# Slots zeroed during the scan, four tiles' statistics at its end, and a re-ordered attention head

## The reference, cut to what matters

```python
x = x + tanh(g_xattn[0]) * mamba(ctx, layernorm(x))     # selective scan, 512 channels x 16 states
x = x + tanh(g_ffn[0])   * moe(layernorm(x))            # 16 experts, top 2, and a shared expert
x = x + tanh(g_xattn[1]) * attention(layernorm(x), ctx) # 32 heads of 16, rotary positions, Wout
x = x + tanh(g_ffn[1])   * ffn(layernorm(x))            # both weights rounded to -1, 0, 1
```

## Time and profile before

| | us |
|---|---|
| three runs, median (lowest to highest) | 1593.91 (1592.81 to 1600.19) |
| the profiled execution | 1594.93 |
| its span, first to last instruction | 1593.1 |
| PE, DVE, ACT, POOL busy | 1457.8, 1136.2, 969.9, 531.4 |

### The profile page before, as it was taken

How to read it: one execution, slowest core, us unless ns; L and a number is a source line. 1 busy time by engine, 2 the same in 40 slices (tenths; PEclk the granted TensorE clock), 3 DMA queues, 4 the chain that set the end, 5 groups by cost and what they waited for, 6 DMA issues and landing times. The chain is left out here.

```text
span 1593.1 us, 21411 instructions
## 1 busy us (share of the span) xinstructions
PE 1457.8 (92%) x6233; PEld 635.7 (40%) x6245; DVE 1136.2 (71%) x1673; ACT 969.9 (61%) x1527; POOL 531.4 (33%) x343
## 2 busy tenths in 40 slices
PE   5788988889978999999999788899999999989999
PEld 2334434444434444444444343332333333334444
DVE  7899999999995422222223757788989999737885
ACT  3999999999934011111111532477787887877764
POOL 0679788698961630000003645705000000000000
PEclk7799989989989999999999889999999999999999
DMA  5202102003473484457524626354323233120464
GB/s 188 64 25 58 49 21 74 20 15 80 151 245 141 165 219 156 145 203 263 187 90 139 219 80 178 117 181 122 81 72 95 72 84 83 59 106 14 81 140 123
DMA packets 141799, 183.41 MB, mean 115 GB/s; under 512 B 54771, under 2 KB 88947, under 8 KB 140707
## 3 DMA queue, kind: packets, MB, share of 16 engines
q1 hardware_dynamic: 120198, 134.58, 28.7%
q0 software_dynamic: 6624, 23.14, 4.7%
q10 hardware_dynamic: 14912, 24.89, 4.7%
HBM read 109.29 MB, written 54.92 MB: 103 GB/s over the span
## 5 line engine op out<-in xcount | busy, mean ns | idle before, releaser
L1814 DVE TENSOR_REDUCE a_mx<-a_s 128x2 f32<-128x1024 f32 x256 | 303.5, 1218 | 33.9 <-PE a_s L1928 30.4
L267 POOL TENSOR_TENSOR m_hs<-m_hs,m_C 128x1024 f32<-128x1024 f32 x128 | 302.2, 2379 | 74.9 <-DVE m_hs L474 74.4
L474 DVE TENSOR_TENSOR_SCAN m_hs<-m_dA,m_d 128x512 f32<-128x512 f32 x256 | 293.4, 1199 | 6.9 <-PE m_d L625 6.1
L625 PE MATMUL m_d<-ident_sb,m_dBuT 128*128 128x128 f32 x1024 | 161.8, 290 | 25.1 <-DVE m_hs L474 20.7
L625 PEld LDWEIGHTS m_d<-ident_sb,m_dBuT 128*128 128x128 f32 x1024 | 116.9, 146 | 153.6 <-DVE m_hs L474 86.3
L373 ACT ACTIVATE m_dA<-m_dt,m_negA 128x512 f32<-128x512 f32 x256 | 168.2, 711 | 6.3 <-DVE m_hs L474 3.8
L1252 PE MATMUL e_gu<-e_w,e_xgT 128*128 x376 | 169.1, 592 | 0.0
L351 ACT ACTIVATE m_dBuT<-m_dtuT,m_BT 128x512 f32<-128x512 f32 x241 | 157.8, 711 | 0.1
L1928 PE MATMUL a_s<-ring_sb 96*128 96x512 bf16 x512 | 150.8, 384 | 5.7 <-DVE a_mx L1814 4.7
L920 ACT ACTIVATE e_sg<-e_gu 128x256 f32<-128x256 f32 x47 | 18.0, 383 | 222.9 <-PE e_gu L1252 222.9
L640 PE MATMUL m_y<-m_hs,m_fold 128*64 128x512 f32 x512 | 142.9, 639 | 0.4 <-POOL m_hs L267 0.4
(11 more groups left out here) (329 smaller groups left out, 2424.1 us busy)
## 6 DMA issues: line engine op xcount, KB each, us to landing
e_w<-in_ex_gu SPq DMA_DIRECT2D x16, 1024.0 KB, 6.2
ring_sb<-qk_dram SPq DMA_DIRECT2D x64, 192.0 KB, 3.1
xg_dram<-zeros_sb SPq DMA_DIRECT2D x2, 6016.0 KB, 28.3
e_xg<-xg_dram ACTq DMA_DIRECT2D x47, 256.0 KB, 2.7
yg_dram<-attn_sb ACTq DMA_DIRECT2D x47, 256.0 KB, 2.0
m_C<-c_dram SPq DMA_DIRECT2D x64, 128.0 KB, 2.9
m_dt<-m_dt SPq DMA_DIRECT2D x64, 128.0 KB, 2.3
e_w<-in_ex_dn SPq DMA_DIRECT2D x16, 512.0 KB, 7.6
```

The lines of the kernel that those rows point to most:

```text
L267: pool.tensor_tensor(hs[:, J % RH], hs[:, J % RH], C2[:, N % RC].unsqueeze(1).broadcast_to([P, 2, L]), ALU.mult).then_inc(s_hc, 1)
L474: dve.tensor_tensor_scan(hs[:, J % RH, h], dA[:, j % RA], pd[j % RD][:], 0.0, ALU.mult, ALU.add)\
L625: last = pe.transpose(pd[j % RD][:, t * P:(t + 1) * P], dBuT[:, N % 2, t, g], ident[:])
L1814: dve.tensor_reduce(mx[:, r % 2, h * TB + 2 * c:h * TB + 2 * c + 2], psc[c][:], AX.X, ALU.max)\
```

## The change

1. **Zeros.** The two DMAs behind the last C load are gone. From the fifth `load_c` on, each is followed by one or two DMAs that zero one slot (256 KB) each, 47 in all over 28 loads. POOL's wait before the scatter counts 47 DMAs.
2. **First chunk's layer norm.** At the end of `mamba`'s list ACT sums the four tiles of batch 0 (Identity with an accumulated output), negates and scales the sums to minus the mean, sums squares of x - mean, and takes the root; DVE adds a reciprocal and a product ahead of its last gate and add. `moe` takes these columns: ACT begins with the four normalisations, DVE with the statistics of tiles 4 and 5, and copies of chunk 0 alternate with the statistics of 6 and 7; `columns(1)` moves ahead of the statistics of 8 and 9.
3. **Shared weights.** One semaphore for each of the three; PE waits for gate, up and down where each is first used.
4. **Attention head.** POOL's inverse roots of batches 0 and 1 follow the gathers of tiles 7 and 11. `inverse(3)` stands ahead of `rotate(0)` on DVE, `normalise(3)` ahead of item 0 on ACT, the turning of batch 3 at n = 1 on PE.
5. **First maxima.** DVE splits them, right behind the last maxima of the group (n = 8 and n = 12), with the `split` that its loop already uses. At n = 10 PE projects the first half, turns the maxima, projects the second half, and then waits for the turned maxima's copy.

```diff
             def load_c(N):
 ...
+                if N == RC:
+                    sp.wait_ge(s_z0, 1)
+                for j in range(zeroed(N), zeroed(N + 1)):
+                    sp.dma_start(xg_dram[j].rearrange("p (c d) -> p c d", c=2),
+                                 zeros[:].unsqueeze(1).broadcast_to([P, 2, D // 2])).then_inc(s_zero, 16)
+            def zeroed(N):
+                return max(N - RC, 0) * ST // (B * PAIRS - RC)
 ...
-            for c in range(2):
-                sp.dma_start(xg_dram.rearrange("j p d -> p j d")[:, :, c * D // 2:(c + 1) * D // 2],
-                             zeros[:].unsqueeze(1).broadcast_to([P, ST, D // 2])).then_inc(s_zero, 16)
 ...
+            act.wait_ge(s_add, E4)
+            for t in range(TB):
+                if t >= 1:
+                    act.wait_ge(s_lead, t)
+                act.activation(junk[:], x_sb[:, t], ACT.Identity, accum_out=lead[:, 0, t:t + 1]).then_inc(s_lead, 1)
+            act.wait_ge(s_lead, TB)
+            act.activation(lead[:, 0], lead[:, 0], ACT.Copy, scale=-1.0 / D).then_inc(s_lead, 1)
+            for t in range(TB):
+                act.wait_ge(s_lead, TB + t + 1)
+                act.activation(junk[:], x_sb[:, t], ACT.Square, bias=lead[:, 0, t:t + 1], accum_out=lead[:, 1, t:t + 1])\
+                    .then_inc(s_lead, 1)
+            act.wait_ge(s_lead, 2 * TB + 1)
+            act.wait_ge(s_eps, 1)
+            act.activation(lead[:, 1], lead[:, 1], ACT.Sqrt, scale=1.0 / D, bias=lead[:, 2, 0:1]).then_inc(s_lead, 1)
 ...
             for et in range(E4 - 1):
                 add(B - 1, et)
+            dve.wait_ge(s_lead, 2 * TB + 2)
+            dve.reciprocal(lead[:, 1], lead[:, 1]).then_inc(s_lead, 1)
+            dve.wait_ge(s_lead, 2 * TB + 3)
+            dve.tensor_tensor(lead[:, 0], lead[:, 0], lead[:, 1], ALU.mult).then_inc(s_lead, 1)
             gate_sum(B - 1, E4 - 1)
 ...
-            root(0)
-            normalise(0)
+            for t in range(TB):
+                act.activation(xn[:, t], x_sb[:, t], ACT.Identity, scale=lead[:, 1, t:t + 1], bias=lead[:, 0, t:t + 1])\
+                    .then_inc(s_xn, 1)
 ...
-            statistics(0, 1, 2, 3)
-            variance(0)
-            columns(0)
             statistics(4, 5)
-            copy_x(0, 1, 2, 3)
-            statistics(6, 7)
+            copy_x(0)
+            statistics(6)
+            copy_x(1)
+            statistics(7)
+            copy_x(2)
             variance(1)
+            copy_x(3)
+            columns(1)
             statistics(8, 9)
-            columns(1)
 ...
-            pe.wait_ge(s_ws, 16 * 3)
+            pe.wait_ge(s_ws[0], 16)
             shared_block(0, 0)
             turn_x(4, 5)
             turn_logits(0)
+            pe.wait_ge(s_ws[1], 16)
             shared_block(0, 1)
 ...
-                if t in (8, 12):
-                    inverse_root(t // TB - 2)
+                if t in (7, 11):
+                    inverse_root(t // TB - 1)
 ...
-                if n in (FIRST + 4, FIRST + 8):
-                    split((n - FIRST - 4) // G4)
 ...
+            normalise(3)
             for n in range(ITEMS - 1):
-                if n == 1:
-                    normalise(3)
 ...
             variance(3)
+            inverse(3)
             rotate(0)
-            inverse(3)
 ...
                     maxes_of(0, g, h, 1)
+                    if h == G4 - 1:
+                        split(0, g)
 ...
                 if n == 1:
                     turn_x(2)
-                if n == 2:
                     turn_x(3)
 ...
+                project(n, 0)
                 if n == FIRST + 5:
                     pe.wait_ge(s_zero, 1)
                     pe.wait_ge(s_mx, 9)
                     turn(0, 0, pmt_early)
-                project(n, 0)
-                if n == FIRST + 5:
+                    project(n, 1)
                     pe.wait_ge(s_mc, 1)
```

More of the change, by code:

```diff
@@ L33, with mamba @@
 LN_READY = 2 * NT + 3
-def mamba(nc, x_sb, ident, identb, tg, a, c_dram, xg_dram, zeros, s_zero):
+def mamba(nc, x_sb, ident, identb, tg, a, c_dram, xg_dram, zeros, s_zero, lead):
     G8 = 2 * E4
@@ L61, in mamba @@
         w_xp = sb("w_xp", [P, E4, RX])
+        junk = sb("junk", [P, D])
         w_dt = sb("w_dt", [R, D])
@@ L102, in mamba @@
         s_cst = sem("c_stored")
+        s_eps = sem("epsilon_set")
+        s_lead = sem("first_layer_norm_steps")
         s_d2 = [sem(f"dt_doubled{i}") for i in range(E4)]
@@ L231, in _ @@
             pool.memset(zeros[:], 0.0).then_inc(s_z0, 1)
+            pool.memset(lead[:, 2], EPS).then_inc(s_eps, 1)
             def scale_first(et):
@@ L712, with moe @@
 GR = 8
-def moe(nc, x_sb, ident, tg, a, xg_dram, yg_dram, s_zero, early, s_early, attn, s_tab, slot, wk, tab_dram, yo, s_yst):
+def moe(nc, x_sb, lead, ident, tg, a, xg_dram, yg_dram, s_zero, early, s_early, attn, s_tab, slot, wk, tab_dram, yo, s_yst):
     with ExitStack() as ctx:
@@ L794, in moe @@
         s_wg = sem("gate_weights_loaded")
-        s_ws = sem("shared_weights_loaded")
+        s_ws = [sem(f"shared_{n}_loaded") for n in ("gate", "up", "down")]
         s_pad = sem("gate_weights_padded")
@@ L840, in _ @@
             sp.dma_start(iota[:], a["iota"].partition_broadcast(P)).then_inc(s_w, 16)
-            sp.dma_start(ws2[:], a["sh_down"].rearrange("(k p) e -> p k e", p=P)).then_inc(s_ws, 16)
+            sp.dma_start(ws2[:], a["sh_down"].rearrange("(k p) e -> p k e", p=P)).then_inc(s_ws[2], 16)
             def load_expert(e, r):
@@ L898, in _ @@
             pool.wait_ge(s_slot, 1)
-            pool.wait_ge(s_zero, 32)
+            pool.wait_ge(s_zero, 16 * ST)
             for k in range(2):
@@ L924, in root @@
             def root(c):
-                act.wait_ge(s_var, c + 1)
+                act.wait_ge(s_var, c)
                 act.activation(rstd[:, c * TB:(c + 1) * TB], rstd[:, c * TB:(c + 1) * TB], ACT.Sqrt).then_inc(s_sd, 1)
             def normalise(c):
-                act.wait_ge(s_nm, c + 1)
+                act.wait_ge(s_nm, c)
                 for t in range(c * TB, (c + 1) * TB):
@@ L1023, in columns @@
                 r = rstd[:, c * TB:(c + 1) * TB]
-                dve.wait_ge(s_sd, c + 1)
+                dve.wait_ge(s_sd, c)
                 dve.reciprocal(r, r).then_inc(s_ln, 1)
@@ L1289, in _ @@
             shared_up(3)
+            pe.wait_ge(s_ws[2], 16)
             for n in range(4, NB):
@@ L1631, in part_3 @@
                     .then_inc(s_p3, 1)
[L1633 to L1644, removed]
             for n in range(2):
@@ L2026, in _ @@
                     scores(0, g, h, 0)
-                project(n, 1)
+                if n != FIRST + 5:
+                    project(n, 1)
                 if 0 <= g < 2:
@@ L2515, in build @@
         s_zero = ctx.enter_context(nc.semaphore("slots_zeroed"))
-        mamba(nc, x_sb, ident, identb, tg, a, c_dram, xg_dram, zeros, s_zero)
+        lead = ctx.enter_context(nc.sbuf_tensor("lead_sb", [P, 3, TB], F32))
+        mamba(nc, x_sb, ident, identb, tg, a, c_dram, xg_dram, zeros, s_zero, lead)
         early = ctx.enter_context(nc.sbuf_tensor("early_sb", [P, KD * T], F32))
@@ L2520, in build @@
         yo = attn[:].rearrange("p i t c -> p (i t c)")[:, (NT - 2) * D:NT * D].rearrange("p (a d) -> p a d", a=2)
-        moe(nc, x_sb, ident, tg[:, 2:3], a, xg_dram, yg_dram, s_zero, early, s_early, attn, s_tab, slot, wk, tab_dram, yo, s_yst)
+        moe(nc, x_sb, lead, ident, tg[:, 2:3], a, xg_dram, yg_dram, s_zero, early, s_early, attn, s_tab, slot, wk, tab_dram, yo, s_yst)
         mark = ctx.enter_context(nc.semaphore("first_after_moe"))
```

6 lines of the change are left out of this document (2 added, 4 removed).

## The result

The changed kernel took 1584.61 us (median of 7 runs, 1582.01 to 1589.26); the kernel before, in the same group, 1597.01 (7 runs, 1592.81 to 1600.59). The ratio is 0.9928, 95% interval 0.9909 to 0.9946: 0.7% faster, where 1.0% was forecast. The profiled execution took 1584.61 us with a span of 1582.6, against 1594.93 and 1593.1: 10.3 us by the times and 10.5 by the spans, where the sum said 16.2. In medians the gain is 12.4 us. The forecast of 1577.7 was counted from 1593.9, the median of three runs of the kernel before; in this group that kernel took 3.1 us more.

The account below looks back on a forecast made before the run. DVE and ACT nearly fill the scan; elsewhere PE sets the pace, losing time idle and at half clock. Terms +0.3 -4.2 (including +0.4) -3.3 -5.8 -3.2 = -16.2 us from 1593.9 gave 1577.7, say 1578; range 1569 to 1590.

Parts of the forecast that it names:

- Zeros in the scan: Scan's batch borders: 256 KB zeros delay ACT 1.3 us three times, mostly covered by slack; +0.3 us, bounds 0 and 4.
- The slack of 6.5 us: Scan: ACT made the decays by 161.5, DVE needs them only at 167.98, so later ACT copies would mostly be absorbed.
- Statistics: Scan's end: ACT's early sums hidden in its free time, DVE's two small instructions not hidden; +0.4 us, bounds 0 and 1.0.
- Expert head: Expert block's start: earlier normalisation and turning, logits at 472.7, shared block at 474.6, clock rising near 477; -4.2 us.
- Rival (d): Expert and attention heads: PE's clock stays at 2.4 GHz in both, giving 1571 us; chance 0.09.
- Attention head: Attention block's start to item 2: earlier roots and batch 3 turning bring item 2's rotation forward; -3.3 us, bounds 0 and -6.4.
- The tie at the first operand load: Attention head: item 1's operand load lands at 944.4 as PE reaches first scores at 944.3; 0.3 us charged.
- Items 8 to 15: Attention items: DVE's split costs 0.72 us and is ready early, removing PE's gaps at n = 10 (-5.8) and 14 (-3.2).
- the bound of -6 for the pair: n = 10 and 14 together: smallest gain, if DVE's added work and item 10's chain eat a third; other bound -10.2.
- Rival (a): Attention head and items: waits return at the first operand load (+3) and n = 10 (+3), giving 1584 us; chance 0.19.
- Rival (b): SP's queue at scan borders: dt2 copies held behind zeros, 21 us per border, giving 1641 us; chance 0.07.
- rival (c): Scan and both heads: ACT stays 4 us behind, heads give less, no change that shows, 1589 us; chance 0.15.

Follow-up runs that it names:

- again: The changed kernel itself, unaltered, timed once more in a later group as yardstick: median 1597.29 us, 0.9909 of the kernel before.
- a_fill: Changed kernel, but POOL's two subtractions beside each early split of maxima only write zeros: one execution 1589.39 us, kernel before 1612.23.
- a_late: Changed kernel, each early split behind the next item's rotation, PE projecting both halves of items 10 and 14 before the turning: one execution 1588.84 us, before 1612.23.
- a_pool: Changed kernel with the early splits back on POOL, PE's new order at item 10 kept: one execution 1595.27 us, kernel before 1612.23.
- after: First profiled execution of the changed kernel, all parts of the change in: 1584.61 us against 1594.93 for the kernel before.
- x_lead: Kernel before plus only the early statistics, the expert head using them and separate shared-weight waits: one execution 1602.25 us, kernel before 1614.04.
- late5: Same code as a_late, timed against the kernel before: median 1591.79 us, ratio 0.9871.
- late_zend: late5 with the slots zeroed in two large DMAs at the scan's end: median 1588.47 us, 0.9861 of the kernel before.

## Why the forecast held, and where its working was wrong

**Zeros in the scan (+0.3).** The cost at a border was right: 0.60 us of issue, 1.3 us more wait on average over three (1.1, 0.9, 2.0). What it does to the end was not: starts with zeros (8 kernels, 466.65 to 469.44) average 467.75, without (5, 465.76 to 467.26) 466.50, so about 1.2 us. With a scatter as wide as that the mean is weak evidence for the size; that something gets through is shown by the waits of PE for ACT's scaled inputs. The slack of 6.5 us was that of the decays; ACT's other products, which PE needs, had less.

**Statistics (+0.4).** Covered on ACT; DVE's two operations took 0.17 and 0.16 us and put about 0.3 us between the last adds and the last gate. Right.

**Expert head (-4.2).** Measured -5.0 at the second turning, -5.9 within the stretch. Logits and shared block came within 0.1 us of the times forecast, though by two errors that cancel: the block started 0.5 us late, and the way from there to the logits took 6.15 us instead of 6.6. The clock's rise near 477 was met too; the value was a compromise with the case in which it rose later. But in again, a_fill, a_late and a_pool the clock was still up for the logits, which took 1.06 us instead of 1.93, and the stretch was 10.2 to 10.7 us instead of the 12.6 to 12.8 of after, x_lead, late5 and late_zend. Rival (d) is met in this head as often as the forecast, and worth 2 us more.

**Attention head (-3.3).** Measured -4.0, and over all kernels 89.8 (4 with the old order) to 86.1 (9 with the new): -3.7. The tie at the first operand load was won: no wait for a load is in the trace there. The gap ahead of batch 3's turning is 3.01 us, at the short end of the 3 to 5 named.

**Items 8 to 15 (-5.8 and -3.2).** This is the step of the prediction that failed, and it carried 9.0 of its 16.2 us, in the words "the split costs DVE 0.72 us and is ready long before PE asks". It costs 4.5 us, since DVE's instructions there are held by POOL's subtractions. At n = 10 PE waits 1.65 and 2.04 us and runs four matmuls at half clock (3.32 instead of 1.88, 1.4 us), 5.1 of the 7.1 us that were to go: -2.1. At n = 14 the 3.14 us became 1.99, and the clock fell behind them in this trace and not in the one of before: +0.5. Together -1.5 instead of -9.0 (-3.0 with the same clock on both sides). My row for the duration came from a stretch in which POOL was idle, and the bound of -6 for the pair rested on the same 0.72 us; the one split of before that ran beside POOL would have given 4.6 us. With the hold shortened (a_fill) the items gave 7.7 us of the 9.0, and with the split in a gap of POOL (a_late, with another order on PE) 9.0. Rival (a) had the right place ("gives n = 10 only two thirds") for another reason.

The sum of -16.2 missed 7.5 us here, and 2 us of unasked gains in the two heads gave part of it back; the measured time is 1584.6 in a range of 1569 to 1590. It is also rival (a)'s 1584, by coincidence: its first half, a lost tie at the operand load, did not happen. That the forecast held is owed in part to luck and to the width of the range: the sign and the gains of both heads were right, and more than half of the sum was not. Rival (b) fell: no scan waited longer for decays than before (0.4 us). So did rival (c): in the first two traces what the heads gained all reached the end (373.61 and 373.47 us, 570.7 and 570.9).

## What to carry to other kernels

A duration is a duration beside certain neighbours. Before an instruction is moved to VectorE, read what GpSimd does in the stretch where it will stand: two operations of 0.17 us each took the rest of a subtraction of 2.1 us, and the spread of that line over the whole trace (174 to 1184 ns before) had shown that it could be held. Take work out from behind a busy engine in time, not only in queue. And where two waits end at nearly the same time, ending one gains only the difference: here ready statistics and landed weights were 1 us apart, and both had to go.

## What the runs showed of the hardware

- A small DVE operation with two SBUF inputs is held while a POOL subtraction runs (1.98 us for 0.17) and is free beside a POOL fill (0.18); a `TENSOR_SCALAR` and a cast to bf16 over 128x16 are held by the fill too (0.96 and 0.70). DVE's rotation multiplies keep their 1.22 us beside a subtraction (the one at 962.79 in the changed kernel, with POOL at work from 961.62); of their two inputs one is PE's product in PSUM.
- TensorE's granted clock behind one and the same gap differs from execution to execution: behind 3.14 us it stayed at 1.00 once and fell in four other kernels (3.65 us for eight matmuls or 5.35 to 6.53), and behind 1.99 to 2.00 us it fell twice and stayed up twice (5.35 or 3.65), once each in the changed kernel itself. A difference of 2 us between two traces can be that alone; the gap's length in the stretch ahead is the steadier number.
- A write of 256 KB of zeros cost SP 0.60 us of issue and held the copies behind it 0.9 to 2.0 us in all, 1.3 on average, which is what the rate of the large zeros had given.
